# A two-layer graph-attention kernel on one core: the second layer's last source scores taken from the first layer's output, its late rows made beside the last matrix products

## The chip, the cores and the metric

The kernel runs on one core of one Trainium2 chip. The metric is the device time of one execution in microseconds (us); lower is better. Of the kernel before, three executions were timed, and one further execution was recorded by the hardware profiler.

## The reference

The input is a graph of N = 1250 nodes and 20,000 random edges, with x of 1250 x 768. Two graph-attention layers run one after the other, then the residual and a layer norm:

```
h = (x @ W).reshape(N, H, C)                 # layer 1: 4 heads of 512; layer 2: 1 head of 768
al_s = einsum(h, a_src); al_d = einsum(h, a_dst)
e = leaky_relu(al_s[src] + al_d[dst], 0.2)   # edges and self loops
m = segment_max(e, dst)                      # over the sources of each target
alpha = exp(e - m[dst]) / (segment_sum(exp(e - m[dst]), dst) + 1e-16)
out = segment_sum(h[src] * alpha, dst) + bias
```

Layer 1 ends with elu, and its output (1250 x 2048) is layer 2's input. The result is layernorm(x + layer 2).

## The kernel before, in words

**Form of the work.** The edges are turned into a dense table of counts C (1250 x 1250). Attention is then dense: for each pair of a source block b (10 blocks of 125 nodes) and a half g of the targets (625 each) a tile of weights P is made, `min(exp(...), 1) * C`, and TensorE accumulates P^T @ [h, 1] in PSUM over b. Such a tile is a *chunk*, number c: chunks 0 to 79 are layer 1 (4 heads x 2 halves x 10), 80 to 99 are layer 2 (80 to 89 the first half, 90 to 99 the second). Float32 products are made of three products of a high and a low part (lines 1726 to 1728, helper `products`), so each chunk passes these steps, with the semaphore that each gives:

- ScalarE `act_relu`: relu(UP * (d + s)) from the target row `drow` and the source's own score (`z_done`)
- GpSimd `pool_add`: plus the shift row `grow` (`e_done`)
- ScalarE `act_exp` (`p_done`), VectorE `dve_counts` (`pc_done`), ScalarE `act_hi` and VectorE `dve_lo` for the two parts (`pt_hi`, `pt_lo`)
- TensorE: 15 pieces of three products.

ScalarE's order is hi(c), exp(c+1), relu(c+2), and in layer 2 also the high part of block c+1 of h2 (`split_h2`). There are three buffers for a chunk in work.

**Order of the heads.** Each engine has its own program, written out by hand, and waits on semaphores; there is no scheduler. In the second half (g = 1) of heads 0 to 2 VectorE also takes the next head's masked maxima (`maxima`, two for each of five chunks) and TensorE makes a block of the next head's h after each chunk. All transfers are issued by SyncE, in one order. The shift of the next head goes through memory: `store_shift` writes `gcol` as a column, and `load_grow` reads it back as a row on all partitions.

**Between the layers (W2 stage).** For each block b of 10: the layer-1 rows come from memory (`load_hb` to `hblk`, two slots); TensorE transposes them in two halves (`transpose_h`), ScalarE and VectorE make the parts `hT`; TensorE multiplies by W2 (`mm_half(2b)`, `mm_half(2b+1)`: 8 steps k of 6 products); ScalarE takes h2 out of PSUM (`h2_out`, line 1167); VectorE takes its source and target scores (`scores2`, line 1520, two instructions with an accumulator, into `al2`). The source score of each block is stored as a column and read back as a row piece of `arow2` (`store_s2`, `load_s2`). With that row VectorE takes the layer's masked maxima: blocks 0 to 3 at once (`maxima2`, line 1530), blocks 4-5, 6-7 and 8-9 in three parts of ten instructions (`part_maxima2`, line 1545, `merge`, line 1553).

**At the end of the W2 stage,** after the last product: h2_out(9), scores2(9), TensorE spreads the score of block 9 over all partitions (`spread`, line 1792: one product with the identity per block of 125), ScalarE copies it (line 1214), the third part of the maxima, `merge`, `dve_shift` (lines 641 to 645), a spread of the 10 target scores (copied by lines 1190 to 1192 to `drow2`), a spread of the shifts (copied by lines 1197 and 1198 to `grow2`), and then chunk 80's steps.

**Layer 2.** TensorE takes chunks 80 to 89 all into the eight banks (`ORDER2`), then waits for target tiles 0 and 1 to be evicted (`evict2`, line 1606, semaphore `y_b`) and takes the second half tile by tile. On VectorE evict2(0) and evict2(1) stand before dve_lo(97). The last steps are layer norms (`norm`, lines 1623 to 1632), and the stores of the output.

## Time and profile before

| what | value |
|---|---|
| median of 3 runs | 937.47 us (936.48 to 937.52) |
| the profiled execution's own time | 937.02 us |
| its span, first to last instruction | 935.1 us |
| mean granted TensorE clock | 0.987 |
| busy: TensorE, VectorE, ScalarE, GpSimd | 881.1, 602.1, 424.4, 198.1 us |
| transfers | 111.18 MB, 119 GB/s on average |

The times above are of whole executions; the profile's span leaves out 1.9 us around them. A busy TensorE means that some product was in flight, not that it ran at its peak. Lines are those of the kernel before. The changed kernel has other line numbers, since lines were added.

### The profile page before, as it was taken

Reading aid. Unit: us, or ns where it says so; the run is one execution under the profiler, and the core shown is the slowest. Engines: PE = TensorE matmul, PEld = TensorE weight load, DVE = VectorE, ACT = ScalarE, POOL = GpSimd, SP = SyncE. Lnnn points to the kernel's source line nnn. Section 1 sums busy time; section 2 is a strip of 40 time slices with the busy share of each in tenths; the row PEclk is TensorE's granted clock in tenths of the full one; section 3 lists DMA queues with packets and bytes.
Section 4 is the critical chain, followed back from the end, with each engine's and each line's share of the span. In section 5 each row is a group of like instructions: output and inputs, shape, how many; then the busy total and the mean of one; then the engine's idle time right before and its main releaser. Section 6 shows DMA issues by size and latency. Waiting matters only on the chain.

```text
span 935.1 us, 15156 instructions
## 1 busy us (share of the span) xinstructions
PE 881.1 (94%) x5719; PEld 796.9 (85%) x5719; DVE 602.1 (64%) x1169; ACT 424.4 (45%) x686; POOL 198.1 (21%) x134
## 2 busy tenths in 40 slices
PE   4998879999999999999999999989999999699996
PEld 2455557799888998889988899989999999599996
DVE  9458663668873889638895488672223334497886
ACT  5456452276643866339652396661111111487300
POOL 1000000144212332124321244300000000155452
PEclk9999989999999999999999999999999999799999
DMA  8609999462548237472174243655223322400223
GB/s 298 145 14 132 178 174 159 135 211 81 177 138 239 67 103 212 112 231 78 29 214 139 68 142 117 174 166 115 72 48 70 85 48 30 102 1 2 69 84 95
DMA packets 64450, 111.18 MB, mean 119 GB/s; under 512 B 31772, under 2 KB 33464, under 8 KB 63004
## 3 DMA queue, kind: packets, MB, share of 16 engines
q1 hardware_dynamic: 64379, 110.22, 45.7%
q8 instruction: 46, 0.75, 0.4%
q14 instruction: 25, 0.20, 0.1%
HBM read 85.25 MB, written 24.94 MB: 118 GB/s over the span
## 4 chain that ended last, share of the span: by engine, by line
PE 67%; DVE 11%; issue 9%; POOL 6%; ACT 3%; DMA 2%; DVEq 1%; SPq 1%; POOLq 0%; ACTq 0%
PE ps L1726 19%; PE ps L1728 19%; PE ps L1727 19%; POOL pbuf L608 5%; PE ps L1755 3%; PE ps L1696 2%; PE ps L1847 2%; PE ps L1686 1%; DVE pbuf L621 1%; DVE h2f L1632 1%; DMA mask_scratch<-nbs 1%; DVE h2f L1606 1%; DVE vbuf L1440 1%; DMA w1f<-in_L_gnn_W 1%; DVE bnst L1623 1%
## 5 line engine op out<-in xcount | busy, mean ns | idle before, releaser
L608 POOL TENSOR_TENSOR pbuf<-pbuf,grow 125x625 f32<-125x625 f32 x100 | 169.9, 1700 | 701.2 <-ACT pbuf L593 261.1
L1726 PE MATMUL ps<-hx,PThi 125*125 125x260 f32 (+5 forms) x800 | 227.3, 284 | 3.0 <-DVE vbuf L1441 2.5
L1728 PE MATMUL ps<-hx,PTlo 125*125 125x260 f32 (+5 forms) x800 | 225.4, 282 | 0.0
L1727 PE MATMUL ps<-hlo,PThi 125*125 125x260 f32 (+4 forms) x800 | 224.9, 281 | 0.0
L1726 PEld LDWEIGHTS ps<-hx,PThi 125*125 125x125 f32 x800 | 148.7, 186 | 7.0 <-DVE vbuf L1441 2.9
L1727 PEld LDWEIGHTS ps<-hlo,PThi 125*125 125x125 f32 x800 | 149.1, 186 | 1.4
L1728 PEld LDWEIGHTS ps<-hx,PTlo 125*125 125x125 f32 x800 | 149.0, 186 | 0.0
L1726 PE MATMUL ps<-W2p,hT 128*125 128x384 f32 x320 | 109.7, 343 | 3.2 <-DVE hT L1453 1.7
L1728 PE MATMUL ps<-W2p,hT 128*125 128x384 f32 x320 | 108.1, 338 | 0.0
L1727 PE MATMUL ps<-W2p,hT 128*125 128x384 f32 x320 | 108.1, 338 | 0.0
L621 DVE SCALAR_TENSOR_TENSOR pbuf<-pbuf,counts 125x625 f32<-125x625 f32 x100 | 90.7, 907 | 25.3 <-ACT pbuf L615 25.2
L630 ACT ACTIVATE PThi<-pbuf 125x625 fp32r<-125x625 f32 x80 | 57.8, 722 | 106.1 <-PE ps L1728 57.0
L615 ACT ACTIVATE pbuf<-pbuf,s_sl 125x625 f32<-125x625 f32 x100 | 81.2, 812 | 48.9 <-POOL pbuf L608 48.8
L635 DVE TENSOR_TENSOR PTlo<-pbuf,PThi 125x625 fp32r<-125x625 f32 x80 | 77.1, 964 | 40.4 <-ACT PThi L630 40.2
L1453 DVE TENSOR_TENSOR hT<-ps,hT 128x500 fp32r<-128x500 f32 x40 | 25.2, 672 | 108.7 <-ACT hT L1129 108.7
L1726 PE MATMUL ps<-h2x,PT 125*125 125x384 f32 (+9 forms) x250 | 77.6, 310 | 6.2 <-DVE PT L635 4.2
L1129 ACT ACTIVATE hT<-ps 128x500 fp32r<-128x500 f32 x40 | 21.2, 586 | 133.0 <-PE ps L1847 133.0
L593 ACT ACTIVATE pbuf<-drow,s_up 125x625 f32<-125x625 f32 x100 | 80.2, 804 | 0.0
L1727 PE MATMUL ps<-h2lo,PT 125*125 125x384 f32 (+7 forms) x250 | 77.3, 309 | 0.0
L1728 PE MATMUL ps<-h2x,PT 125*125 125x384 f32 (+9 forms) x250 | 77.3, 309 | 0.0
L1728 PE MATMUL ps<-W1hi,xr 128*125 128x512 f32 x180 | 71.1, 395 | 0.0
L1726 PE MATMUL ps<-W1hi,xr 128*125 128x512 f32 x180 | 71.0, 395 | 0.0
(186 smaller groups left out, 1571.6 us busy)
## 6 DMA issues: line engine op xcount, KB each, us to landing
xr<-xT_scratch SPq DMA_DIRECT2D x30, 750.0 KB, 4.9
nbm<-mask_scratch SPq DMA_DIRECT2D x40, 273.4 KB
hidden_scratch<-vbuf SPq DMA_DIRECT2D x40, 224.0 KB
hblk<-hidden_scratch SPq DMA_DIRECT2D x10, 896.0 KB
xT_scratch<-xa SPq DMA_DIRECT2D x20, 375.0 KB, 11.7
w1f<-in_L_gnn_W SPq DMA_DIRECT2D x12, 512.0 KB, 9.1
w1raw<-in_L_gnn_W SPq DMA_DIRECT2D x4, 1536.0 KB, 7.9
w2raw<-in_L_gnn_W SPq DMA_DIRECT2D x14, 384.0 KB, 5.4
```

The lines of the kernel that those rows point to most:

```text
L593: act.activation(pslot(c), src[:, g * GN:(g + 1) * GN], ACT.Relu, scale=UP, bias=bias).then_inc(z_done, 1)
L608: pool.tensor_tensor(pslot(c), pslot(c), src[:, g * GN:(g + 1) * GN], ALU.add).then_inc(e_done, 1)
L615: act.activation(pslot(c), pslot(c), ACT.Exp, scale=SLOPE, bias=bias).then_inc(p_done, 1)
L621: dve.scalar_tensor_tensor(pslot(c), pslot(c), 1.0, C[:, b, g * GN:(g + 1) * GN], ALU.min, ALU.mult).then_inc(pc_done, 1)
L630: act.activation(hi_slot(c), pslot(c), ACT.Copy).then_inc(pt_hi, 1)
L635: dve.tensor_tensor(lo_slot(c), pslot(c), hi_slot(c).bitcast(F32), ALU.subtract).then_inc(pt_lo, 1)
L1129: hi = act.activation(ht_part(n % 2, 0, a), PS[:, bank, 0:4 * B], ACT.Copy)
L1453: lo = dve.tensor_tensor(ht_part(n % 2, 1, a), PS[:, bank, 0:4 * B], ht_part(n % 2, 0, a).bitcast(F32), ALU.subtract)
L1726: pe.matmul(dst, ahi, bhi, start=start, stop=False, skip_group_check=shared)
L1727: pe.matmul(dst[:, 0:n], ahi, blo, start=False, stop=False, skip_group_check=shared)
L1728: return pe.matmul(dst, alo, bhi, start=False, stop=stop, skip_group_check=shared)
L1755: t = pe.matmul(win_bank(w), oh_lo[:, bass.ds(at_slot(first, i, v), 1), :].rearrange("p o n -> p (o n)"), ring[:, w % 2, v, 0:win_cols(w)] ...
```

## The change

**In the heads.** W2 times the source vector a_src of layer 2 is a vector of 2048 numbers, w2a: h2's source score is the layer-1 row times w2a. VectorE makes it in 16 pieces (`FOLD2`): in the second half of head 0 and 1 after its other work of chunks b = 0, 1, 5, 8, 9, of head 2 after b = 0, 1, 5, 7, 8, 9. Each piece is one instruction on 128 x 768 (rows of W2 times `as2row`, with an accumulator), and SyncE loads 384 KB of W2 for it into the one buffer `wf2`, waiting for the piece before. After the last piece w2a is stored.

**In the W2 stage.** `prow` is loaded with w2a in three parts (`load_prow`). VectorE takes the source scores of blocks 8 and 9 from `hblk` times `prow` (`late_dots`, six instructions, `late_scores` sums them). TensorE spreads the source scores of blocks 7, 8, 9 before step 6 of mm_half(17), and ScalarE copies them to `arow2`; the stores and loads of scores 7 and 8 through memory are gone. All three parts of the maxima come in VectorE's turn of block 8, the second before `split_hT(19)` and the third after it. `shift2(0)` makes the shifts of the first half; TensorE spreads them before step 3 of mm_half(19). The first half's target row comes through memory.

**At the end.** h2_out(8) waits for the third part of the maxima, since part of `nbp2` and `prow` lie where blocks 8 and 9 of h2 go. Chunk 80's add is made by VectorE from PSUM. h2_out(9) comes after act_hi(80) on ScalarE; TensorE's first chunk waits for h2 blocks 8 and 9 and the copy of the shifts at the pieces that need their banks. The second half's target and shift rows go through memory.

```diff
+FOLD2 = tuple((h, b) for h in range(H - 1) for b in ((0, 1, 5, 8, 9) if h < H - 2 else (0, 1, 5, 7, 8, 9)))
...
+            def load_fold2(h, b):
+                if (h, b) in FOLD2:
+                    i = FOLD2.index((h, b))
+                    if i > 0:
+                        sp.wait_ge(fold2_done, i)
+                    sp.dma_start(wf2[:], W2[128 * i:128 * i + 128, :]).then_inc(ld_fold2, 16)
...
+                    load_fold2(h, (5, None, 7, None, 8)[t])
                 store_shift(h + 1)
                 load_grow(h + 1, 0)
                 load_xr(h + 1, NB - 2)
+                load_fold2(h, 9)
...
+            for b in range(NB - 3):
+                load_hb(b + 3)
+                sp.wait_ge(al2_done, 2 * b + 1)
+                store_s2(b, b + 1)
+                if b == NB - 4:
+                    load_prow(1)
+                sp.wait_ge(s2_stored, RS * (b + 1))
+                load_s2(b, b + 1, ld_s2[max(0, b // 2 - 1)])
...
+                if b == 5:
+                    load_prow(0)
...
+            load_prow(2)
+            sp.wait_ge(ht_ps, 2 * NB - 2)
+            load_part(1)
+            sp.wait_ge(dot_done, 2 * len(PP) + 1)
+            load_part(2)
...
+                    if b == NB - 2:
+                        act.wait_ge(bc2_ps, 1)
+                        act.activation(arow2[:, (NB - 3) * B:N], PS[0:B, 6, 0:3 * B], ACT.Copy).then_inc(bc2_sb, 1)
                     split_hT(2 * b + 3)
-                h2_out(b)
-
-
-            act.wait_ge(h2_sb, NB)
+                if b == NB - 2:
+                    act.wait_ge(mx_last, QP * NB)
+                if b < NB - 1:
+                    h2_out(b)
...
+                if g == 1 and (h, b) in FOLD2:
+                    i = FOLD2.index((h, b))
+                    dve.wait_ge(ld_fold2, RS + 16 * (i + 1))
+                    dve.wait_ge(fold2_done, i)
+                    dve.scalar_tensor_tensor(wf2junk[:], wf2[:], 1.0, as2row[:], ALU.mult, ALU.mult, accum_out=w2a[:, i:i + 1]).then_inc(fold2_done, 1)
...
+                if b == 6:
+                    late_dots(0)
+                if b == 7:
+                    late_dots(2)
+                    late_scores()
...
+                    if n == 2 * NB - 3 and k == LATE_S:
+                        pe.wait_ge(dot_done, 2 * len(PP) + 1)
+                        pe.wait_ge(ht_lo, 2 * NB - 1)
+                        spread(lambda m: al2[:, 0, m:m + 1], lambda m: (6, (m - NB + 3) * B), NB - 3, NB).then_inc(bc2_ps, 1)
+                    if n == 2 * NB - 1 and k == LATE_G:
+                        pe.wait_ge(g_done, H + 1)
+                        spread(lambda m: gcol[:, H * NB + m:H * NB + m + 1], four_from(4), 0, GT).then_inc(bc2_ps, 1)
```

**Where the instructions stand, TensorE.** The rows below are TensorE's program from the last product of the W2 stage in the kernel before (a row is line, operation, output<-inputs and size, and what it waits for; al2 holds the scores, gcol the shifts, h2x and h2lo the parts of h2).

```order
L1728 MATMUL ps<-W2p_127,hT1_133 125x384
L1792 MATMUL ps<-ident_50,al2_67 125x125 [waits al2_done] x2
L1792 MATMUL ps<-ident_50,al2_67 125x125 x9
L1792 MATMUL ps<-ident_50,gcol_66 125x125 [waits g_done]
L1792 MATMUL ps<-ident_50,gcol_66 125x125 x9
L1726 MATMUL ps<-h2x_158,PT2_3_160 125x256 [waits pt_lo,h2_lo,g2_sb,h2x_one]
```

In the changed kernel the two spreads that are left stand inside mm_half(17) and mm_half(19); this is the one inside mm_half(19), between steps 2 and 3:

```order
L1833 MATMUL ps<-W2p_131,hT1_137 125x384
L1897 MATMUL ps<-ident_50,gcol_66 125x125 [waits g_done]
L1897 MATMUL ps<-ident_50,gcol_66 125x125 x4
L1831 MATMUL ps<-W2p_131,hT1_137 125x384
L1832 MATMUL ps<-W2p_131,hT1_137 125x384
```

So 21 spread products after the last W2 product became 3 and 5 between W2 products, and the last W2 product is now followed by chunk 80's first.

**ScalarE, from its last h2_out on.** Before (hT, arow, drow, grow, pbuf are as in the text above, PT is a chunk's high part):

```order
L1167 ACTIVATE h2f<-ps 125x768 [waits h2_ps] x2
L1214 ACTIVATE arow_154<-ps 125x125 [waits bc2_ps,h2_sb]
L1216 ACTIVATE s_up<-al_67 125x10 [waits al2_done]
L1217 ACTIVATE s_sl<-al_67 125x10
L1190 ACTIVATE drow_145<-ps 125x500 [waits bc2_ps]
L1191 ACTIVATE drow_145<-ps 125x500
L1192 ACTIVATE drow_145<-ps 125x250
L593 ACTIVATE pbuf_146<-drow_145,s_up 125x625 [waits pt_lo,s2_up_sb,d2_sb]
```

And now, from the copy of the three spread scores to the third chunk's relu:

```order
L1228 ACTIVATE h2f<-ps 125x768 [waits h2_ps,mx_last]
L1265 ACTIVATE s_up<-al_67 125x10 [waits dot_done]
L1266 ACTIVATE s_sl<-al_67 125x10
L608 ACTIVATE pbuf_155<-drow_154,s_up 125x625 [waits ld_drow0,pt_lo,s2_up_sb]
L608 ACTIVATE pbuf_155<-drow_154,s_up 125x625 [waits pt_lo]
L1272 ACTIVATE h2x<-ident 125x10x2 [waits h2_ps,h2_sb]
L1262 ACTIVATE h2x<-h2f 125x768
L630 ACTIVATE pbuf_155<-pbuf_155,s_sl 125x625 [waits e_done]
L1277 ACTIVATE grow_153<-ps 125x500 [waits bc2_ps]
L1278 ACTIVATE grow_153<-ps 125x125
L645 ACTIVATE PT_1_162<-pbuf_155 125x625 [waits pc_done]
L1228 ACTIVATE h2f<-ps 125x768 [waits h2_ps]
```

Chunk 80's relu, exp and high part (L608, L630, L645) now stand ahead of the last h2_out (the second L1228), where before they stood behind it.

**VectorE, from the end of the maxima on, in the changed kernel:**

```order
L1613 TENSOR_TENSOR mx<-mx,mxp 125x10 [waits mx_all,mx_last]
L1641 SCALAR_TENSOR_TENSOR mneg<-mx,al_67 125x5 [waits al2_done,mx_all]
L1643 SCALAR_TENSOR_TENSOR negm<-mneg 125x5 [waits m_neg]
L1645 SCALAR_TENSOR_TENSOR gcol<-negm,al_67 125x5 [waits m_sb]
L1579 SCALAR_TENSOR_TENSOR a2junk,al_67<-h2f,a2row 125x768 [waits al2_done,h2_sb]
L1686 TENSOR_TENSOR pbuf_155<-pbuf_155,ps 125x500 [waits bc2_ps,z_done]
L1687 TENSOR_TENSOR pbuf_155<-pbuf_155,ps 125x125
L1682 TENSOR_TENSOR h2lo<-h2f,h2x 125x768 [waits h2_hi]
L636 SCALAR_TENSOR_TENSOR pbuf_155<-pbuf_155,counts 125x625 [waits p_done]
L650 TENSOR_TENSOR PT_1_162<-pbuf_155,PT_1_162 125x625 [waits pt_hi]
L1579 SCALAR_TENSOR_TENSOR a2junk,al_67<-h2f,a2row 125x768 [waits al2_done,h2_sb]
L1641 SCALAR_TENSOR_TENSOR mneg<-mx,al_67 125x5 [waits al2_done,mx_all]
```

Chunk 80 is finished here ahead of block 9's target score (the last L1579), which is followed by the shifts of the second half.

## Rows read from the trace of the kernel before

**Rows 1.** The page's busy times and its chain that ended last, by engine.

```profile
PE 881.1 (94%) x5719; PEld 796.9 (85%) x5719; DVE 602.1 (64%) x1169; ACT 424.4 (45%) x686; POOL 198.1 (21%) x134
...
PE 67%; DVE 11%; issue 9%; POOL 6%; ACT 3%; DMA 2%; DVEq 1%; SPq 1%; POOLq 0%; ACTq 0%
```

**Rows 2.** Windows: busy us (instructions) by engine, granted clock, DMA share, GB/s.

```profile
785.00:799.00 14.00, 13.94 (x80) 13.62 (x78) 5.52 (x35) 0.02 (x1) 0.00 (x0) 1.00 0.21 18
799.00:815.00 16.00, 8.44 (x42) 7.77 (x42) 8.76 (x41) 8.24 (x18) 2.75 (x2) 0.79 0.47 124
```

**Rows 3.** Timeline, PE, 798 to 874: start us, us, operation [idle before <-releaser].

```profile
798.61 0.34 PE L1728 MATMUL ps<-W2p,hT 128*125 128x384 f32 x1
...
801.72 4.08 PE L1792 MATMUL ps<-ident,al 125*125 125x125 f32 x20 [0.40 <-DVE a2junk L1520]
...
815.87 0.55 PE L1726 MATMUL ps<-h2x,PT 125*125 125x256 f32 x1 [4.19 <-DVE PT L635]
```

**Rows 4.** Timeline, ACT, 782 to 816 (same columns).

```profile
798.98 0.81 ACT L1167 ACTIVATE h2f<-ps 125x768 f32<-125x768 f32 x1 [15.12 <-PE ps L1728]
...
814.68 0.80 ACT L615 ACTIVATE pbuf<-pbuf,s_sl 125x625 f32<-125x625 f32 x1
```

**Rows 5.** Timeline, POOL: the add of chunk 82.

```profile
816.26 1.52 POOL L608 TENSOR_TENSOR pbuf<-pbuf,grow 125x625 f32<-125x625 f32 x1 [3.00 <-ACT pbuf L593]
```

**Rows 6.** Timeline, PE, 180 us: ten spread products (two records each).

```profile
180.33 2.42 PE L1792 MATMUL ps<-ident,gcol 125*125 125x125 f32 x20 [1.04 <-DVE gcol L645]
```

**Rows 7.** Timeline, DVE: split_hT(19), then the second part of the maxima.

```profile
783.19 1.27 DVE L1453 TENSOR_TENSOR hT<-ps,hT 128x500 fp32r<-128x500 f32 x2 [5.14 <-ACT hT L1129]
...
786.13 0.41 DVE L1545 CUSTOM_DVE_ANT_0 junk<-nbp,arow 125x250 bf16<-125x250 bf16 x1
...
790.77 0.17 DVE L1553 TENSOR_TENSOR mx<-mx,mxp 125x10 f32<-125x10 f32 x1
```

**Rows 8.** Timeline, DVE: a score of block 7, and the first of block 9.

```profile
766.64 0.95 DVE L1520 SCALAR_TENSOR_TENSOR a2junk<-h2f,a2row 125x768 bf16<-125x768 f32 x1
...
799.82 0.96 DVE L1520 SCALAR_TENSOR_TENSOR a2junk<-h2f,a2row 125x768 bf16<-125x768 f32 x1 [8.88 <-ACT h2f L1167]
```

**Rows 9.** Timeline, SP: block 6's scores as a column, then back as a row.

```profile
748.15 0.74 SPq L852 DMA_DIRECT2D score_scratch<-al  x2
757.31 0.74 SPq L858 DMA_DIRECT2D arow<-score_scratch  x2
```

**Rows 10.** Timeline, DVE: evict2(0) begins.

```profile
869.87 0.15 DVE L1594 TENSOR_SCALAR deps<-ps 125x1 f32<-125x1 f32 x1
```

**Rows 11.** Timeline, PE: the second half's first product.

```profile
873.14 0.46 PE L1726 MATMUL ps<-h2x,PT 125*125 125x384 f32 x1 [1.99 <-DVE h2f L1606]
```

**Rows 12.** Waits, 190 to 640: us in total, times, longest us.

```profile
ACT PThi L630 <- PE ps L1728: 57.0, 21, 3.1
...
PE ps L1726 <- DVE PTlo L635: 0.3, 1, 0.3
```

**Rows 13.** Windows, the busiest part of a second half-pass (columns as in rows 2).

```profile
244.00:260.00 16.00, 16.00 (x100) 14.20 (x99) 15.73 (x24) 8.30 (x13) 3.70 (x3) 1.00 0.76 232
873.00:877.00 4.00, 3.86 (x13) 3.86 (x14) 3.21 (x4) 1.35 (x2) 3.93 (x2) 0.57 0.53 171
```

**Rows 14.** Timeline, head 2's second half: DVE, SP, POOL, DVE, ACT.

```profile
487.54 2.04 DVE L1447 SCALAR_TENSOR_TENSOR vbuf<-ebuf,vbuf 125x512 f32<-125x512 f32 x1
...
500.95 0.93 SPq L723 DMA_DIRECT2D shift_scratch<-gcol  x2
509.46 0.76 SPq L717 DMA_DIRECT2D grow<-shift_scratch  x2
...
513.72 1.53 POOL L608 TENSOR_TENSOR pbuf<-pbuf,grow 125x625 f32<-125x625 f32 x1 [16.38 <-DMA grow<-shift_scratch]
...
517.32 0.69 DVE L1339 TENSOR_TENSOR hlo<-ps,hx 125x512 fp32r<-125x512 f32 x1 [0.37 <-ACT hx L995]
...
524.17 0.73 ACT L630 ACTIVATE PThi<-pbuf 125x625 fp32r<-125x625 f32 x1 [3.02 <-PE ps L1728]
```

216 lines of the change are left out of this document (136 added, 80 removed).

## The prediction

> **What bounds the kernel now.** First the page: TensorE has work in flight for 94% of the span and holds 67% of the chain that ended last [rows 1]. Whatever is gained must come from where it has none. Second the windows: from 799 to 815 us TensorE is busy for 8.44 of 16 us at a granted clock of 0.79, the one long hole outside the start, and right before it for 13.94 of 14 [rows 2]. Third the timeline of that hole: the last W2 product starts at 798.61, then come spreads and waits, the last of them 4.19 us for the first chunk, whose first product starts at 815.87 [rows 3]. The spreads run slow there: 20 records take 4.08 us, and 2.42 at 180 us [rows 3, 6]; the granted clock of 0.79 is a mix of the full 2.4 GHz and the lower level of 1.2 [rows 2].
>
> Then I ask what ends last behind the hole. TensorE takes the first half of layer 2 from 815.87 until 871.15 (873.14 less the 1.99 of idle), and waits for evict2(1) [rows 3, 11]. On VectorE the evictions stand at a fixed place, before dve_lo(97), and evict2(0) begins at 869.87, when TensorE has long left that tile [rows 10]. So **the start of the second half is set by the chunk loop of ScalarE, GpSimd and VectorE, not by TensorE's first half**; from there to the end every engine follows. An earlier first product alone is worth nothing beyond that: the chunk loop has to begin earlier. Its periodic part begins with chunk 82's add on GpSimd, at 816.26 [rows 5]; chunk 97's evictions follow 53.6 us later. That distance stays: same instructions, same three buffers.
>
> **The change, part by part.**
>
> *1. What stands between the last W2 product and chunk 82's add.* Before: h2_out(9) starts on ScalarE at 798.98, the add at 816.26, 17.28 us later [rows 4, 5]. After: ScalarE does h2_out(9), exp(81), relu(82), and GpSimd adds; chunk 80 is done before. Before, the score starts 0.84 after h2_out's start (799.82 less 798.98) [rows 4, 8], which I take for the step to exp(81) as well; from exp(81) to the add it is 816.26 − 814.68 = 1.58 [rows 4, 5]. So 2.42 us instead of 17.28: **14.86 gained**.
>
> *2. What the W2 stage gains in length.* Three and five spread products inside mm_half(17) and mm_half(19), at the clock of their neighbours: ten blocks take 2.42 at full clock [rows 6], eight take 1.94. **1.94 lost.** Bounds: at the slow pace of the first spread it would be 8/10 of 4.08, 3.3 [rows 3]; the low end is 1.9, since the work itself is needed.
>
> *3. Waits for those spreads.* Scores: the six dots and their sum come when VectorE is idle for 5 us at a time (before split_hT(19) it sat 5.14 [rows 7]). I cost them at nothing, and their cover is nearly 10 us: block 7's second score starts at 766.64 and takes 0.95 [rows 8], late_dots(2) adds two shorter ones: 769.5. Counted back from 798.8 at 13.94/80 = 0.174 us a product [rows 2], two halves of 48, two steps of 6 and some 0.9 of transposes, the spread before step 6 of mm_half(17) stands at 779. This leans on prow(1) and prow(2) landing in time behind block 9's load. A column with that load ahead of it took 748.15 to 757.31, 9.2 us [rows 9]; with 9 us instead of my 3 for each, the cover is gone and the wait is up to about 3 us (late_dots(0) at 757, twice 9, the dots and the sum, against 779).
> Shifts: the three-score copy is there at about 780.5 (779, 0.73 of spread, 0.8 for copy and handoffs). Second part of the maxima: 786.13 to 790.77, 4.64 [rows 7], so here from 780.5 to 785.3 with its merge; split_hT(19), 1.27 [rows 7], starts there instead of at 783.19 (its user, mm_half(19), starts at 791, so over 4 us of cover); third part 4.64, merge and shift2(0) 0.8: 792.1. The spread stands before step 3 of mm_half(19): 798.8 less 30 products, plus the first spread's 0.73, 794.3. **Cover about 2 us, cost nothing**; anything later than that is paid one to one.
>
> *4. Chunk 80.* The second spread is done at 795.5. VectorE's add, exp, counts, high part (beside the copies of the shifts) and low part follow, five steps of some 0.85 each (an exp takes 0.80 [rows 4]): about 799.8, against the end of W2 at 798.95 + 1.94 = 800.9. **TensorE starts at once**, with 1.1 us of cover; were it a little late, the end would not move, since the loop hangs on h2_out(9). Behind h2_out(9) VectorE has scores2(9) (0.96 [rows 8]) and shift2(1) before counts(81): some 0.7 late against the old spacing, while chunk 82's add does not wait for it.
>
> *5. The heads.* 16 instructions of 0.95 us (a score is the same form [rows 8]), 15.2 us of VectorE, and 6.3 MB more. In 190 to 640 us TensorE waited once, 0.3 us, for a low part, while ScalarE waited 57 us for TensorE to free a buffer [rows 12]: VectorE is ahead. I cost them at nothing. The thin spot is head 2: the shift goes out at 500.95, is back at 509.46 and is added at 513.72; the block of h behind it is split on VectorE at 517.32, and TensorE comes for it when chunk 58 is done, about 524.2 (ScalarE's buffer wait ends then) [rows 14]. The loads of pieces 14 and 15 stand ahead in SyncE's queue, the former behind a wait for VectorE; I make the delay 4 to 5 us, with 6.6 of cover.
> In the same stretch a 512-column instruction took 2.04, where another of that width takes 0.69 [rows 14]: 1.35 more. At 2.3 a piece, 16 make 37 us instead of 15.2, and the four among maxima would leave VectorE up to 5 us behind; that is the first rival's upper end, and for that I give it 0.05 more. The Trainium skill, "SBUF — State Buffer", section "Who interferes with whom", has it that a VectorE instruction with two SBUF inputs and a GpSimd one that reads SBUF contend for a shared pair of ports, and the one that comes second waits for the other to end. The trace agrees with it in that row.
>
> *6. Second half.* TensorE now finishes its first half at 800.9 + 55.3 − 1.5 (no slow clock at its start) = 854.7, and VectorE lets it go on at 873.14 − 12.9 = 860.2: it idles 5.5 us instead of 2. After 1.99 idle the clock stood at 0.57 for 873 to 877 [rows 13], so that loss is paid already; I take the same loss after the longer gap; no row shows it, and twice the loss, 1.6 us more, is my bound.
>
> **Sum:** 14.86 − 1.94 = 12.9 us. Against the profiled execution's 937.02: 924.1; the median of the runs lies 0.45 above that execution: **924.6**.
>
> **Rivals.**
> - *The folds cost TensorE something.* Loads and port waits push head 2's shift past its 6.6 us, or a piece of W2 lands late and VectorE stands before a needed low part. For it: VectorE is busy 15.73 of 16 us in 244 to 260 [rows 13], where b = 5 falls. Against: VectorE is ahead [rows 12]. 1 to 5 us back: 925.6 to 929.6. Chance 0.15.
> - *A spread comes late in the W2 stage* (point 3): 1 to 5 us: 925.6 to 929.6. Chance 0.10.
> - *TensorE sets the end after all:* if the loop runs faster than before and VectorE reaches its evictions by 854.7, the gain is 871.15 − 854.7 = 16.4: 921.0. Against: the loop's add-exp-relu circle has no part that the change shortens. Chance 0.05.
> - *Slower:* VectorE becomes the engine that sets the pace of the second half-passes, and all 16 pieces are paid. It decides once VectorE has no idle time left per chunk and is no longer ahead; the row of 244 to 260 comes near that, but only 4 of the 16 pieces lie in chunks with maxima. 924.6 + 15.2 = 939.8. Chance 0.03.
> - *It does not do what it says:* a wait in SyncE's single queue (block 9's load, dots, prow, maxima) closes in a row, and chunk 80 begins where it did: 936 to 937.5. Chance 0.02.
>
> **Numbers.** The forecast has 0.65. A measurement of this kernel tells about 0.2% (1.9 us) from no change: faster 0.95, same 0.02, slower 0.03. Range: from 921.5 (most of the faster rival, and 3 us for a step I priced too high) to 929.5 (both rivals of late waits).
>
> **What would show it.** h2_out(9) at about 801 and chunk 82's add 2.4 us behind it; TensorE's first layer-2 product within 0.5 us of its last W2 product, at full clock; no wait at the two spreads; evict2(0) near 857; TensorE idle for about 5.5 us before the second half; low parts still ahead in the heads, chunk starts there unmoved. Wrong if TensorE waits over 1 us for gcol or for the scores, or if mm_half(0) starts later than before.

## The result, and the profile after

The changed kernel takes 926.65 us, median of 4 runs (925.62 to 928.05), against 936.98 of the kernel before (4 runs, 936.31 to 937.52) in the same comparison: a ratio of 0.988, 95% interval [0.986, 0.99]. Two later comparisons gave 0.9882 [0.9859, 0.9906] and 0.9866 [0.9838, 0.9894]. Its profiled execution took 926.86 us, its span 924.8 (before: 937.02 and 935.1). The forecast of 924.6 is 2.05 us too low.

First the page's busy times and its chain that ended last, the lines that answer to [rows 1].

```profile
PE 876.1 (95%) x5693; PEld 792.6 (86%) x5693; DVE 621.3 (67%) x1215; ACT 422.2 (46%) x681; POOL 205.3 (22%) x133
...
PE 69%; DVE 11%; issue 8%; POOL 6%; ACT 3%; DMA 1%; DVEq 1%; SPq 0%; POOLq 0%; ACTq 0%
```

Then windows in the columns of [rows 2]: the end of the W2 stage, and what was the hole. TensorE is busy for all of the first, at full clock, and for 11.40 of 12 us in the first chunks of layer 2, where [rows 2] had 8.44 of 16 at 0.79. The third window is the beginning of the second half.

```profile
785.00:799.00 14.00, 14.00 (x85) 14.00 (x85) 10.60 (x56) 4.76 (x10) 0.00 (x0) 1.00 0.00 0
803.00:815.00 12.00, 11.40 (x95) 11.18 (x94) 11.20 (x13) 10.09 (x14) 5.92 (x3) 1.00 0.07 2
861.00:867.00 6.00, 4.22 (x13) 4.22 (x14) 5.92 (x8) 1.39 (x2) 4.54 (x3) 0.50 0.39 128
```

The timeline of TensorE (start us, us, operation [idle before <-releaser]), as in [rows 3]: the score spreads (six records), the shift spreads, the last W2 product, the first product of layer 2, the wait for chunk 81, and the second half's first product.

```profile
780.85 0.82 PE L1897 MATMUL ps<-ident,al 125*125 125x125 f32 x6
...
796.08 1.25 PE L1897 MATMUL ps<-ident,gcol 125*125 125x125 f32 x10
...
802.26 0.34 PE L1833 MATMUL ps<-W2p,hT 128*125 128x384 f32 x1
802.43 0.28 PE L1831 MATMUL ps<-h2x,PT 125*125 125x256 f32 x1
...
808.57 0.38 PE L1831 MATMUL ps<-h2x,PT 125*125 125x256 f32 x1 [0.60 <-DVE PT L650]
...
862.78 0.68 PE L1831 MATMUL ps<-h2x,PT 125*125 125x384 f32 x1 [5.64 <-DVE h2f L1712]
```

Neither spread waits, and the first product of layer 2 starts 0.17 us after the last W2 product starts. Next are ScalarE, GpSimd and VectorE, for [rows 4, 5, 10]. The first ScalarE row is h2_out(9), the GpSimd row is chunk 82's add, and the last VectorE row is evict2(0). The VectorE rows before it are the wait for prow(1), the sum of the scores, the last step of shift2(0) and the low part of chunk 80:

```profile
802.63 0.81 ACT L1228 ACTIVATE h2f<-ps 125x768 f32<-125x768 f32 x1 [1.85 <-PE ps L1833]
803.48 0.82 ACT L630 ACTIVATE pbuf<-pbuf,s_sl 125x625 f32<-125x625 f32 x1
804.20 0.81 ACT L608 ACTIVATE pbuf<-drow,s_up 125x625 f32<-125x625 f32 x1
...
805.08 1.90 POOL L623 TENSOR_TENSOR pbuf<-pbuf,grow 125x625 f32<-125x625 f32 x1 [3.56 <-ACT pbuf L608]
...
767.05 0.96 DVE L1627 SCALAR_TENSOR_TENSOR a2junk<-hblk,prow 125x768 bf16<-125x768 f32 x1 [5.21 <-DMA prow<-folded_scratch]
...
775.25 0.16 DVE L1633 TENSOR_REDUCE al<-bnst 125x2 f32<-125x6 f32 x1
...
793.64 0.17 DVE L1645 SCALAR_TENSOR_TENSOR gcol<-negm,al 125x5 f32<-125x5 f32 x1
...
800.81 1.37 DVE L650 TENSOR_TENSOR PT<-pbuf,PT 125x625 fp32r<-125x625 f32 x1 [0.80 <-ACT PT L645]
...
859.52 0.15 DVE L1700 TENSOR_SCALAR deps<-ps 125x1 f32<-125x1 f32 x1
```

From h2_out(9) to chunk 82's add it is now 805.08 − 802.63 = 2.45 us, where [rows 4, 5] have 17.28. Yet evict2(0) comes only 10.35 us earlier (859.52 for 869.87), and that is not all the loop's doing: the first shifts' spread, in a stretch that the change does not touch, starts here at 182.45, 2.12 us later than in [rows 6]. It has to be known whose these 2.12 us are before anything else is counted.

**One reference point.** In every trace that follows I count from the first eviction of head 0, a VectorE row of form 125x260 that stands near 227 us in all kernels and that the change leaves alone. Three landmarks behind it: the last such eviction of the heads, evict2(0), evict2(2) (the third eviction of the last stage), and the span's end. All numbers are differences of starts in one trace.

| profiled execution | first head eviction at | last head eviction | evict2(0) | evict2(2) | end |
|---|---|---|---|---|---|
| kernel before | 227.54 | +385.12 | +642.33 | +654.33 | +707.56 |
| changed | 229.69 | +384.89 | +629.83 | +641.91 | +695.11 |
| changed, e4_changed_again | 225.59 | +384.85 | +629.82 | +641.92 | +695.11 |
| changed, e12_changed_base | 230.19 | +384.84 | +629.77 | +641.86 | +695.11 |

Behind the reference point three executions of the changed kernel agree to 0.06 us; ahead of it they differ by 4.6. Counted so, the change gains 12.50 us at evict2(0) and 12.45 at the end.

### The profile page after: what moved, and what is told of

Same layout as the page of the kernel before. It is cut to its first block, busy times and chain, and to the rows that moved or that the text cites. A ratio compares the mean times of both kernels' runs of the same rounds, so it can differ in the third digit from the quotient of the medians.

```text
span 924.8 us, 15200 instructions
## 1 busy us (share of the span) xinstructions
PE 876.1 (95%) x5693; PEld 792.6 (86%) x5693; DVE 621.3 (67%) x1215; ACT 422.2 (46%) x681; POOL 205.3 (22%) x133
## 4 chain that ended last, share of the span: by engine, by line
PE 69%; DVE 11%; issue 8%; POOL 6%; ACT 3%; DMA 1%; DVEq 1%; SPq 0%; POOLq 0%; ACTq 0%
PE ps L1831 19%; PE ps L1833 19%; PE ps L1832 19%; POOL pbuf L623 6%; PE ps L1860 4%; PE ps L1801 3%; PE ps L1952 2%; PE ps L1791 1%; DVE h2f L1738 1%; DVE pbuf L636 1%; DVE h2f L1712 1%; DMA w1f<-in_L_gnn_W 1%; DVE bnst L1729 1%; DVE vbuf L1495 1%; DVE vbuf L1494 1%
## 5 line engine op out<-in xcount | busy, mean ns | idle before, releaser
L623 POOL TENSOR_TENSOR pbuf<-pbuf,grow 125x625 f32<-125x625 f32 x99 | 177.1, 1790 | 683.0 <-ACT pbuf L608 244.3
L630 ACT ACTIVATE pbuf<-pbuf,s_sl 125x625 f32<-125x625 f32 x100 | 81.3, 813 | 59.0 <-POOL pbuf L623 56.9
L636 DVE SCALAR_TENSOR_TENSOR pbuf<-pbuf,counts 125x625 f32<-125x625 f32 x100 | 88.2, 882 | 28.5 <-ACT pbuf L630 28.3
L645 ACT ACTIVATE PThi<-pbuf 125x625 fp32r<-125x625 f32 x80 | 57.8, 722 | 107.1 <-DVE pbuf L636 64.5
L650 DVE TENSOR_TENSOR PTlo<-pbuf,PThi 125x625 fp32r<-125x625 f32 x80 | 83.5, 1043 | 28.2 <-ACT PThi L645 28.2
L608 ACT ACTIVATE pbuf<-drow,s_up 125x625 f32<-125x625 f32 x100 | 80.3, 805 | 0.0
## 6 DMA issues: line engine op xcount, KB each, us to landing
xT_scratch<-xa SPq DMA_DIRECT2D x20, 375.0 KB, 10.4
```

What stands on the lines that cost most here:

```text
L608: act.activation(pslot(c), src[:, g * GN:(g + 1) * GN], ACT.Relu, scale=UP, bias=bias).then_inc(z_done, 1)
L623: pool.tensor_tensor(pslot(c), pslot(c), src[:, g * GN:(g + 1) * GN], ALU.add).then_inc(e_done, 1)
L630: act.activation(pslot(c), pslot(c), ACT.Exp, scale=SLOPE, bias=bias).then_inc(p_done, 1)
L636: dve.scalar_tensor_tensor(pslot(c), pslot(c), 1.0, C[:, b, g * GN:(g + 1) * GN], ALU.min, ALU.mult).then_inc(pc_done, 1)
L645: act.activation(hi_slot(c), pslot(c), ACT.Copy).then_inc(pt_hi, 1)
L650: dve.tensor_tensor(lo_slot(c), pslot(c), hi_slot(c).bitcast(F32), ALU.subtract).then_inc(pt_lo, 1)
```

## The experiments

Times of whole runs differ by several us from execution to execution, so the effects of 0.3 to 4 us below are read in the landmarks; the timed ratio stands beside each. The three comparisons ran with medians of 938.05, 939.95 and 937.53 us for the kernel before.

**e4_changed_again and e12_changed_base** are the changed kernel without an edit.

> The changed kernel itself once more, timed beside the kernel before, as the base of the other runs of this call. If the 2.1 us that its profiled execution had lost by the first shifts' spread (182.45 against 180.33 us) is the execution's own, the spread stands elsewhere this time by up to 2 us and the whole later trace with it; if it belongs to the program, it stands at 182.4 +- 0.3 us. Ratio to the kernel before 0.988 +- 0.002 either way.

> The changed kernel once more, as the base of the runs of this call on their chip. Counted from the first head eviction (near 227 us) its landmarks are those of the two traces of it so far to 0.2 us: first eviction of the last stage +629.8, third +641.9. What lies ahead of the first head eviction may differ by some us, as in the runs so far (the first shifts' spread at 178.2 to 184.8 us).

Measured 925.6 us, ratio 0.9882 [0.9859, 0.9906], and 925.5 us, 0.9866 [0.9838, 0.9894]. The first shifts' spread starts at 178.38 and 182.98. So the 2.12 us are the execution's own. Over all fourteen traces of this study that spread lies between 178.16 and 184.84, whichever kernel it is. The windows show one difference that goes with it: the stretches in which TensorE's clock was granted below full. First the changed kernel, then e4:

```profile
60.00:80.00 20.00, 16.84 (x105) 11.94 (x104) 11.82 (x43) 11.36 (x25) 0.00 (x0) 0.91 0.37 69
...
120.00:140.00 20.00, 12.89 (x74) 8.79 (x72) 13.00 (x44) 11.44 (x24) 0.00 (x0) 0.91 1.10 195
140.00:160.00 20.00, 19.17 (x90) 14.92 (x91) 6.53 (x20) 4.88 (x9) 0.00 (x0) 0.83 0.73 149
```

```profile
60.00:80.00 20.00, 16.64 (x119) 11.88 (x117) 13.56 (x49) 12.21 (x27) 0.00 (x0) 1.00 0.41 68
...
120.00:140.00 20.00, 12.77 (x73) 8.55 (x72) 15.06 (x50) 10.41 (x21) 0.00 (x0) 0.89 1.10 195
140.00:160.00 20.00, 20.00 (x99) 15.84 (x99) 5.35 (x10) 5.50 (x10) 0.00 (x0) 0.94 0.99 164
```

The six other windows of 20 us up to 180 are at 1.00 in both. An estimate from these rows: 20 us times what the clock lacks of full, summed up to 180 us, is 7.0 us in the changed kernel and 3.4 in e4, where the spread comes 4.07 us earlier. Over the fourteen traces this sum goes from 3.4 (spread at 178.16 to 180.47) to 10.4 (184.84). So the late starts go with a longer time at the lower clock, but it is not all: five traces besides e4 have the same 3.4, the kernel before among them, and they differ by 2.3 us. This is read from the rows and not tested; what makes the clock fall there, and what the rest is, stays open.

**e1_folds_alone**: the kernel before with the folds only.

```diff
+                load_fold2(h, 0)
...
+                if g == 1 and (h, b) in FOLD2:
+                    i = FOLD2.index((h, b))
+                    dve.wait_ge(ld_fold2, RS + 16 * (i + 1))
+                    dve.wait_ge(fold2_done, i)
+                    dve.scalar_tensor_tensor(wf2junk[:], wf2[:], 1.0, as2row[:], ALU.mult, ALU.mult, accum_out=w2a[:, i:i + 1]).then_inc(fold2_done, 1)
```

> The kernel before with the first part of the change alone: the 16 loads of W2 rows, the 16 products of them with the source vector on VectorE in the heads, and the store of the folded column. Nothing reads the result, so all else is the kernel before. Theory (the folds lie in cover): the head evictions of the heads (the 125x260 ones, at 227.54 to 608.73 us in the kernel before) keep their places to 0.3 us but for one constant that is there before the first fold, and the time is the kernel before's, 0 +- 1 us. Rival (the folds cost TensorE in the heads): the evictions drift later from head to head, +1 to +15 us by 608.73. Rival for the 2.1 us by which the changed kernel is late already at the first shifts' spread (182.45 against 180.33 us): if the larger program or the placing of its buffers does it, the spread stands at 182.4 here too; if it is the run's own, it stands anywhere from 180 to 183.

Measured 936.7 us, ratio 0.999 [0.9972, 1.0007]. First head eviction 226.21, last +385.09, evict2(0) +642.64, end +707.89. The heads are as before (+385.12), and so is the start of the last W2 product (+571.04 for +571.07). The 0.3 us are lost behind it: layer 2's first product comes at +588.65 for +588.33. The folds as placed cost TensorE nothing in the heads, and the spread at 178.99 says again that the program is not what makes the start late.

**e7_folds_twice**: how much more VectorE could take.

```diff
-                    dve.wait_ge(fold2_done, i)
-                    dve.scalar_tensor_tensor(wf2junk[:], ...)
+                    for j in range(2):
+                        dve.wait_ge(fold2_done, 2 * i + j)
+                        dve.scalar_tensor_tensor(wf2junk[:], ...)
```

> The changed kernel with each of the 16 folds done twice on VectorE (the second writes the same numbers). VectorE was busy 340.5 of the 450 us from 190 to 640 and gets 16 more of 0.96 to 1.9 us. Theory (the folds lie in VectorE's idle time, and its lead on TensorE absorbs what does not): head evictions at the same distances from the first shifts' spread to 0.3 us, time within 0.5 us of the changed kernel; TensorE's waits for the low parts from 190 to 640 us stay under 1 us. Rival (the single folds had used up the lead): +2 to +16 us, seen as drift from one head eviction to the next.

Measured 928.27 us, ratio 0.9894 [0.9864, 0.9923]. Last head eviction +389.21: 4.3 us later than +384.89, so my theory is refuted at twice the number, and the rival holds in its lower half. Waits from 190 to 640 us (us in total, times, longest), of the changed kernel and then of e7:

```profile
ACT PThi L645 <- PE ps L1833: 42.5, 14, 3.1
...
DVE wf2junk L1550 <- DMA wf<-in_L_gnn_W: 9.0, 6, 3.2
...
PE ps L1831 <- DVE PTlo L650: 0.3, 1, 0.3
```

```profile
ACT PThi L645 <- PE ps L1834: 18.2, 6, 3.1
...
PE ps L1832 <- DVE hlo L1393: 3.3, 4, 2.1
...
PE ps L1832 <- DVE PTlo L650: 0.3, 1, 0.3
```

The row to look at is not the low parts of the chunks, on which the prediction had rested: it stays at 0.3 us. A new one is there: TensorE, about to make the next block of h, waits 3.3 us in all for VectorE to have split the block before it (hlo). The longest of the four waits is in head 2's second half, at the thin spot that point 5 of the prediction names:

```profile
525.94 0.50 PE L1832 MATMUL ps<-W1hi,xr 128*125 128x512 f32 x1 [2.07 <-DVE hlo L1393]
```

The four waits make 3.3 of the 4.3 us; the last us was not followed. ScalarE's wait for TensorE to free a buffer, the measure of how far the helpers are ahead, goes from 57.0 [rows 12] over 42.5 with 16 folds to 18.2 with 32. The single folds had used a part of the lead, and no wait for hlo is in the changed kernel's trace.

**e6_shift_spread_last**: the five shift spreads behind the last W2 product.

```diff
-                    if n == 2 * NB - 1 and k == LATE_G:
-                        pe.wait_ge(g_done, H + 1)
-                        spread(lambda m: gcol[:, ...], four_from(4), 0, GT).then_inc(bc2_ps, 1)
...
                 t.then_inc(h2_ps, 1)
+                if n == 2 * NB - 1:
+                    pe.wait_ge(g_done, H + 1)
+                    spread(lambda m: gcol[:, ...], four_from(4), 0, GT).then_inc(bc2_ps, 1)
```

> The changed kernel with the five spreads of the shifts behind the last W2 product instead of beside the last block: what their place among the products is worth by itself. Theory: the last product ends 1.25 us earlier, the spreads end at about 802.6 us (on the changed kernel's clock of events), VectorE's add of chunk 80 begins at 802.8 instead of 797.44, its exp at 803.7, its high part at 805.4, and the last output copy, which ScalarE has behind them, at 806.1 instead of 802.63; chunk 82's add at about 808.5 instead of 805.08. So +3.4 us (3.0 to 3.8) at the first eviction of the last stage. Rival (the end of the W2 products sets the start, not chunk 80): -1.25 to 0 us. Rival by the old arrangement, in which 14.8 us were lost behind the last output copy: over +6 us, which would say that the place of the spreads is most of the gain.

Measured 929.39 us, ratio 0.989 [0.9863, 0.9917]. evict2(0) +633.59, 3.76 later than in the changed kernel; end +698.95, 3.84 later. TensorE's spreads and its first layer-2 product, ScalarE's exp(80), in e6:

```profile
803.63 1.25 PE L1897 MATMUL ps<-ident,gcol 125*125 125x125 f32 x10
809.79 0.55 PE L1831 MATMUL ps<-h2x,PT 125*125 125x256 f32 x1 [4.91 <-DVE PT L650]
...
805.89 0.82 ACT L630 ACTIVATE pbuf<-pbuf,s_sl 125x625 f32<-125x625 f32 x1 [7.18 <-DVE pbuf L1687]
...
808.22 0.79 ACT L1228 ACTIVATE h2f<-ps 125x768 f32<-125x768 f32 x1
```

ScalarE waits 7.18 us for chunk 80's sum, h2_out(9) stands behind chunk 80's high part, and TensorE is idle for 4.91. The chain is the one expected, 0.4 us longer.

**e9_both_spreads_last**: the score spreads too.

```diff
-                    if n == 2 * NB - 3 and k == LATE_S:
-                        pe.wait_ge(dot_done, 2 * len(PP) + 1)
-                        pe.wait_ge(ht_lo, 2 * NB - 1)
-                        spread(lambda m: al2[:, 0, m:m + 1], ...).then_inc(bc2_ps, 1)
...
                 if n == 2 * NB - 1:
+                    pe.wait_ge(dot_done, 2 * len(PP) + 1)
+                    spread(lambda m: al2[:, 0, m:m + 1], ...).then_inc(bc2_ps, 1)
                     pe.wait_ge(g_done, H + 1)
```

with the row copy on ScalarE and part_maxima2(1) on VectorE behind their split_hT(19).

> The changed kernel with both sets of spreads, the three score rows and the five shift rows, behind the last W2 product. VectorE's part maxima 1 and 2, which read the score rows, then lie behind it too. The row copy on ScalarE and the parts on VectorE are moved behind the last splits, so that the last half block's operands don't wait for them. What the place of the score spreads is worth by itself, beside e6_shift_spread_last (+3.8 us). Theory (the chain score rows, part maxima, shifts, shift rows, chunk 80 lies bare behind the last product): last product at about 800.5 us on the changed kernel's clock of events, score spreads 0.8, row copy 0.5, two parts of 4.65 and their merges, shifts 0.6, shift spreads 1.25, so that VectorE's add of chunk 80 begins at about 813.5 instead of 797.44 and chunk 82's add at about 819 instead of 805.08: +14 us (13 to 15) at the first eviction of the last stage, of which 10 are the score rows'. Rival (most of the gain is that less work is done at all, the products of the last rows being gone): under +8 us.

Measured 941.34 us, ratio 1.0042 [1.0022, 1.0062]: slower than the kernel before. evict2(0) +646.21, 16.4 later than in the changed kernel, where 14 were expected.

```profile
798.68 0.82 PE L1897 MATMUL ps<-ident,al 125*125 125x125 f32 x6
810.67 2.46 PE L1897 MATMUL ps<-ident,gcol 125*125 125x125 f32 x10 [11.17 <-DVE gcol L1645]
818.04 0.55 PE L1831 MATMUL ps<-h2x,PT 125*125 125x256 f32 x1 [4.91 <-DVE PT L650]
...
810.45 0.17 DVE L1645 SCALAR_TENSOR_TENSOR gcol<-negm,al 125x5 f32<-125x5 f32 x1
```

The place of the score rows is worth 16.4 − 3.8 = 12.6 us, that of the shift rows 3.8. Of the 2.4 us over what was expected 1.2 are in one row: the five shift spreads (ten records) take 2.46 us here behind 11.17 us of idleness, and 1.25 in e6. e9 is not the old order, though: it has two parts of the maxima behind the last product, where the kernel before had one. The part that is added takes 4.9 us here (800.25 to 805.15), and without it evict2(0) would stand at about +641.3, an estimate, for the +642.33 of the kernel before. Since e9 does only the work of the changed kernel, by this estimate what fell away (13 of 21 spread products) is worth about 1 us, and the rest of the 12.5 us is the order. The folds matter because they make the last scores known before the last products.

**e5_shift_spread_first and e11_score_spread_first**: what a wait inside the W2 stage costs. The diff is e5's; e11 has `0, 3`.

```diff
-LATE_S, LATE_G = 6, 3
+LATE_S, LATE_G = 6, 0
```

> The changed kernel with the five spreads of the shifts ahead of the last half block of W2 products instead of behind three of its steps (3 x 1.06 us). In the changed kernel's trace the shifts are ready at 793.8 us and the last half block begins at about 792.9, so the spreads have a cover of 2.3 us where they stand, and would have to be waited for by 0.9 us here. Theory (TensorE sets the end of the W2 stage, and a wait in it is paid one to one): TensorE idles 0.8 to 1.0 us before these spreads, and the last output copy, chunk 82's add and the first eviction of the last stage all come 0.8 to 1.0 us later, counted from the first shifts' spread near 180 us. Rival (ScalarE's and VectorE's work on chunk 80, which begins 1.4 us earlier here, sets the start of layer 2): 0 or down to -1 us.

Measured 926.0 us, ratio 0.9859 [0.9832, 0.9885]; evict2(0) +630.99, 1.16 later. The wait is the one expected:

```profile
792.05 1.32 PE L1897 MATMUL ps<-ident,gcol 125*125 125x125 f32 x10 [0.88 <-DVE gcol L1645]
```

> The changed kernel with the three score spreads at the begin of their half block of W2 products instead of behind six of its steps (6 x 1.06 us). In the changed kernel's trace the scores are ready at 775.4 us and the bank that the spreads write is read until 777.07, the spreads begin at 780.85, so the cover is 3.8 us, and at the begin of the half block (774.43) the spreads would have to be waited for by 2.6 us. Theory (a wait of TensorE in the W2 stage is paid one to one): TensorE idles 2.4 to 2.8 us before the score spreads, and the first eviction of the last stage comes 2.4 to 2.8 us later. Rival (the cover is the 10 us that the forecast gave, or the wait is taken up again by the rows being there earlier): 0 to 0.5 us.

Measured 931.14 us, ratio 0.9921 [0.9895, 0.9948]; evict2(0) +637.43, 7.6 later and not 2.6. TensorE's spreads and VectorE's first dot on prow(1), then the windows behind the spreads:

```profile
781.40 1.59 PE L1897 MATMUL ps<-ident,al 125*125 125x125 f32 x6 [4.78 <-DVE hT L1507]
...
771.73 0.96 DVE L1627 SCALAR_TENSOR_TENSOR a2junk<-hblk,prow 125x768 bf16<-125x768 f32 x1 [6.59 <-DMA prow<-folded_scratch]
```

```profile
782.00:793.00 11.00, 11.00 (x53) 11.00 (x53) 6.39 (x46) 0.48 (x1) 0.00 (x0) 0.77 0.32 76
793.00:806.00 13.00, 13.00 (x80) 12.96 (x79) 7.05 (x38) 4.45 (x9) 0.00 (x0) 1.00 0.00 0
```

Two things were missing in my sum. In this execution prow(1) is issued at 762.52 and used at 771.73, 9.2 us instead of 7.8 (759.23 to 767.05); the issue itself is 1.3 us later too, with the reference point's 1.95 taken off. VectorE's queue behind it is later against TensorE's stage: the split that reads the bank which the spreads are to write begins 4.40 us behind TensorE's transposes (780.00 and 775.60) instead of 2.15 (775.81 and 773.66), so the wait is 4.78 us and not 2.6. And behind that wait the clock is granted at 0.77 for 11 us, in a stretch that [rows 2] and the changed kernel pass at full clock; the spreads themselves take 1.59 instead of 0.82. Of the 7.6 us 4.78 are the wait and 0.77 the slower spreads; the slow stretch gives most of the 2.05 that are left (0.23 of 11 us is 2.5, with the end of the spreads in it). In these two runs a wait in this stage is paid at least one to one: 1.16 us for 0.88, and 7.6 for 4.78.

**e2_evict_early**: does TensorE's second half set the end?

```diff
-                if c == CHUNKS + 2 * NB - 3:
+                if c == CHUNKS + 2 * NB - 4:
                     evict2(0)
                     evict2(1)
```

> The changed kernel with the evictions of the first two blocks of the last stage, which free the banks for the second half of layer 2, one chunk earlier in VectorE's order (before the low part of chunk 96 instead of chunk 97). Theory (VectorE's own queue sets the end from there on: its low part of chunk 99, then evictions and norms back to back from 871.6 us to the end): TensorE's second half begins 2 to 3.2 us earlier, at about 859.6 to 860.8 us instead of 862.78, the low part of chunk 99 and the third eviction stay at 871 to 872 us, and the time changes by 0 to -0.5 us. Rival (the begin of the second half on TensorE sets the end): -2 to -3 us.

Measured 925.43 us, ratio 0.9877 [0.9854, 0.99]. TensorE's second half starts at 857.64, +630.05 from the reference point; in the changed kernel it is 862.78, +633.09. That is 3.04 us earlier, and its idle time is down from 5.64 to 2.56:

```profile
857.64 0.68 PE L1831 MATMUL ps<-h2x,PT 125*125 125x384 f32 x1 [2.56 <-DVE h2f L1712]
```

evict2(2) comes at +641.64, 0.27 us earlier, the end 0.20 earlier. So 3 us of TensorE's time before its second half are worth 0.2 us at the end; VectorE's place is what counts. From evict2(2) to the end of the span it is 53.2 us in both kernels (707.56 − 654.33 and 695.11 − 641.91). VectorE's evictions and norms fill it but for ten waits of some 0.67 us for GpSimd's `rstd` and the last 3 us of the output's store, the same in both.

**e3_exp_first, e8_combined, e10_combined_2**: where the loop starts.

```diff
             act_hi(act, CHUNKS)
+            act_exp(act, CHUNKS + 1)
+            act_relu(act, CHUNKS + 2)
             h2_out(NB - 1)
             act.wait_ge(h2_sb, NB)
-            act_exp(act, CHUNKS + 1)
```

is e3 (and the loop leaves that relu out). e8 adds e2's edit and moves `scores2(NB - 1)` and `shift2(1)` from ahead of VectorE's loop to the end of chunk 81's pass. e10 has them earlier:

```diff
             dve_lo(dve, CHUNKS)
-            scores2(NB - 1)
-            shift2(1)
...
                     dve_counts(dve, c + 1)
+                if c == CHUNKS:
+                    scores2(NB - 1)
+                    shift2(1)
                 if c + 1 < CHUNKS + NB:
                     split_h2(c + 1 - CHUNKS)
```

> The changed kernel with chunk 81's exp and chunk 82's relu placed ahead of the last block's output copy on ScalarE, which stood idle for 1.85 us before that copy while GpSimd had chunk 81 ready at 801.5 us. Theory (the chain of ScalarE's relu, GpSimd's add and ScalarE's exp sets the pace of the chunk loop, so its second add sets where it starts): GpSimd's add of chunk 82 begins at about 803.1 instead of 805.08 us, the output copy 0 to 0.7 us later, the loop's chain keeps its step of 3.2 to 3.65 us, and the time changes by -1.5 to -2.0 us. Rival (TensorE's last W2 product and the output copy behind it set the start of layer 2): the first eviction of the last stage stays at 859.5 us or moves later by up to 0.5, and the time changes by 0 to +0.5 us.

Measured 924.72 us, ratio 0.986 [0.9837, 0.9884]; evict2(0) +629.64, evict2(2) +641.75: 0.16 to 0.19 us. GpSimd's add of chunk 82 does come 1.9 us earlier, and the next one gives it back:

```profile
801.12 1.29 POOL L623 TENSOR_TENSOR pbuf<-pbuf,grow 125x625 f32<-125x625 f32 x1 [1.64 <-ACT pbuf L608]
806.88 1.54 POOL L623 TENSOR_TENSOR pbuf<-pbuf,grow 125x625 f32<-125x625 f32 x1 [4.47 <-ACT pbuf L608]
...
804.66 0.73 ACT L645 ACTIVATE PT<-pbuf 125x625 fp32r<-125x625 f32 x1 [2.04 <-DVE pbuf L636]
```

ScalarE stands 2.04 us before chunk 81's high part, since VectorE does counts(81) only behind the score and the shifts, and these wait for h2_out(9). Both theory and rival fell: the ring had a second gate.

> A version meant to beat both. On the changed kernel: chunk 81's exp and chunk 82's relu ahead of the last output copy on ScalarE (which alone gave -0.15 us: the add of chunk 82 came 1.9 us earlier, but chunk 81's counts on VectorE lay behind the last block's score and the last five shifts, which wait for the output copy, and the next add came 5.76 us behind it instead of 3.54), so that score and the shifts are moved behind chunk 82's counts too; and the first two evictions of the last stage one chunk earlier (which alone gave -0.28 us at the third eviction). Theory (the ring of relu, add, exp and counts sets the start of the loop, and both of its gates have to go): the add of chunk 83 begins 1.7 to 2.1 us earlier than in the changed kernel, counted from the first shifts' spread, and the third eviction of the last stage 1.8 to 2.3 us earlier. Rival (a third gate appears: the stores of the second five shifts and targets, now later, or TensorE's first products): under 0.7 us.

Measured 923.87 us, ratio 0.9843 [0.9819, 0.9867]; evict2(2) +640.90, 1.01 earlier, the end 0.98 earlier (0.27 and 0.20 of it are e2's edit). Chunk 83's add is 1.9 us earlier (804.52 − 227.47, against 808.62 − 229.69), but GpSimd's add of chunk 85 comes only 5.65 us behind that of chunk 84, where the usual step is 3.4 to 3.65. VectorE there, and GpSimd's add beside it:

```profile
806.97 0.94 DVE L1580 SCALAR_TENSOR_TENSOR a2junk<-h2f,a2row 125x768 bf16<-125x768 f32 x1
...
808.03 1.40 DVE L1642 SCALAR_TENSOR_TENSOR mneg<-mx,al 125x5 f32<-125x5 f32 x1
809.46 0.17 DVE L1644 SCALAR_TENSOR_TENSOR negm<-mneg 125x5 f32<-125x5 f32 x1
...
807.87 1.53 POOL L623 TENSOR_TENSOR pbuf<-pbuf,grow 125x625 f32<-125x625 f32 x1 [1.64 <-ACT pbuf L608]
```

> As e8_combined (-1.01 us at the third eviction of the last stage), but the last block's score and the last five shifts stand between chunk 81's counts and the low part of h2's block 1 on VectorE, where e8_combined left it idle for 1.47 us, instead of behind chunk 82's work, where they held up chunk 83's counts (GpSimd's fourth add came 5.65 us behind the third). Theory: 0.9 to 1.5 us of those 2.8 us fall into the idle stretch, chunk 83's add begins 0.8 to 1.8 us earlier than in the changed kernel, and the third eviction 1.3 to 2.0 us earlier. Rival (VectorE is the bound of the first ten chunks, 3.6 of 3.65 us of each, and the 2.8 us are paid wherever they stand): -0.8 to -1.2 us, as e8_combined.

Measured 923.27 us, ratio 0.9848 [0.9822, 0.9874], beside 925.5 of the changed kernel in the same comparison; evict2(2) +640.65, 1.26 earlier, end +693.88, 1.23 earlier. It lies at the edge between theory and rival: chunk 83's add is 1.8 us earlier, chunk 84's 0.4, and the loop comes out 1.0 ahead of e2. In its first ten chunks VectorE has low part, counts and h2's low part to do, which fill its step of 3.65 us (records of 0.80, 0.80 and 2.13 us that overlap a little, the last beside GpSimd's add), so work put there is mostly paid. e10 is in the traces the fastest of all, by 1.2 us over the changed kernel; the timed ratios of the two overlap.

## Why the prediction was right, by its steps

All differences here are counted from the reference point, between the traces of before and of the changed kernel.

- **What bounds.** Confirmed by e2: the chunk loop's start and VectorE's place for the evictions set the end; 3 us of TensorE's time before the second half are worth 0.27 at evict2(2). The rival "TensorE sets the end after all" is out.
- **1, 14.86 gained.** Measured 17.28 − 2.45 = 14.83. ScalarE's copy to exp(81) took 0.85 and exp(81) to the add 1.60, against 0.84 and 1.58. e6 and e9 show that it is the order: shift spreads put behind the last product cost 3.8, both sets with their maxima 16.4.
- **2, 1.94 lost.** h2_out(9) stands at +572.94 (802.63 − 229.69) for +571.44 before [rows 4], 1.50 later. The W2 stage had begun 0.24 earlier (its first product that waits, +395.93 for +396.17), so the spreads cost 1.74.
- **3, no waits.** True, and with less room than I gave. Shifts: ready at 793.81, spread at 796.08, 2.3 of cover for my 2. Scores: ready at 775.41, spread at 780.85, 5.4 for my 10, and by e11's bank 3.8. The term that was wrong is the load of prow(1): 3 us in the sum, 7.8 measured here and 7.4 to 9.2 over the twelve traces that have it, near the bound from [rows 9]. That it cost nothing was partly luck. VectorE stood before it for 5.21 us. The second took 4.7 at most (769.04 to 773.78); with 9 us for it too, as in my bound, under 1 us of the cover would have been left (778 for its landing, 780 with the two dots and the sum, against 780.85).
- **4, chunk 80 ready 1.1 us before the end of W2.** 800.81 + 1.37 = 802.18. The last W2 product ends at 802.60, and layer 2's first starts at 802.43: 0.25 to 0.4 of cover. From the end of the spread to there it took 4.85 us, for my 4.3. TensorE still starts at once, as said, at full clock.
- **5, the heads cost nothing.** The last head eviction is even 0.23 us nearer (+384.89 for +385.12; the reason was not looked for). The delay of head 2's shift was my thin spot: store, load, add and split, for [rows 14], stand at

```profile
506.46 1.10 SPq L738 DMA_DIRECT2D shift_scratch<-gcol  x2
514.98 0.76 SPq L732 DMA_DIRECT2D grow<-shift_scratch  x2
...
521.07 1.53 POOL L623 TENSOR_TENSOR pbuf<-pbuf,grow 125x625 f32<-125x625 f32 x1 [22.15 <-DMA grow<-shift_scratch]
...
524.68 0.69 DVE L1393 TENSOR_TENSOR hlo<-ps,hx 125x512 fp32r<-125x512 f32 x1 [0.37 <-ACT hx L1056]
```

  With the reference point's 2.15 off, store and load are 3.4 us later than in [rows 14], add and split 5.2; I had 4 to 5, of 6.6 of cover (by [rows 14] 524.17 − 517.32 − 0.69 = 6.2). Little of it was left: the split ends at 525.37, and the product of TensorE that has to come behind it stands at 526.02, 0.65 us later. That this spot held was luck as much as foresight. The rival "the folds cost TensorE" is out for 16 folds (e1) and true for 32 (e7), where the same product, at 525.94, is the one that waits 2.07 us; the low parts of the chunks, by which I had judged VectorE's lead, show nothing of it.
- **6, the second half.** TensorE idles 5.64 us (5.5 forecast), and the clock is 0.50 for 861 to 867, where [rows 13] have 0.57 behind 2 us. From the first product of the half on, the clock is 0.75 over 6.86 us before (873.14 to 880) and 0.70 over 7.22 us now (862.78 to 870), which makes 1.7 and 2.2 us lost: about the same loss, as forecast, and not twice. The end hangs on VectorE.
- **What was not in the sum.** The chunk loop: 53.6 us from chunk 82's add to evict2(0), "that distance stays", measured 54.44: 0.83 lost. The first three steps of GpSimd's adds are 3.54, 3.65 and 3.65 for 3.18, 3.40 and 3.64 before, 0.62 in all; the score and shifts that point 4 has ahead of counts(81), "some 0.7 late", stand there, and e3 shows that they hold up the ring. The prediction says so in point 4 and leaves it out of the sum. The other 0.2 were not followed.

The sum with what was measured: 14.83 − 1.74 − 0.83 + 0.24 = 12.50, against 12.9; that it is so close owes something to errors of opposite sign (0.83 lost, 0.24 and 0.20 gained). The 2.05 us by which the median was missed are mostly no step of the forecast: 0.45 are steps (12.9 for 12.45 at the end), and 2.15 are the late start of this execution of the changed kernel. Against them stand 0.66, since the median lies 0.21 below its profiled execution where the forecast had it 0.45 above. The rest, 0.1, is outside of the span. The two later comparisons, with six executions each, gave medians of 925.6 and 925.5. Of the rivals, the slower one and the one that it does nothing are excluded by the ratio; "a spread comes late" did not happen, and e11 shows that it would have cost more than one to one.

## What to carry to other kernels

A short instruction put into another engine's stage is worth the chain that had to run behind that engine's last work in the old order. Find the input that is known last, and see whether a product taken beforehand (a fold) makes it known earlier, as with the last scores here. Then take the stall away on paper and ask which queue is the next to hold up the end: here moving one gate (e3) gave 0.2 of 1.9 us, and with the second moved too (e10) and e2's edit it was 1.2. And fix a reference point in the trace behind the noisy start before effects of a few us are counted, since three executions of one kernel differed by 4.6 us ahead of it and by 0.06 behind.

## What the runs showed of the hardware

- **A wait of TensorE in a busy stage cost more than its length.** Behind 4.78 us of idleness the next 11 us had a granted clock of 0.77, a mix of 2.4 and 1.2 GHz, and six spread records took 1.59 instead of 0.82 us (e11). Behind 11.17 us ten records took 2.46 instead of 1.25 (e9), about twice as long, at a granted clock of 0.50 from 810.67 to 813.13. Behind 0.88 us the clock stayed at 1.00 from 791 to 795 (e5), and the last stage still came 1.16 us later.
- **A tiny VectorE instruction can take as long as GpSimd's beside it.** The first step of shift2(1), 125x5 with two inputs in SBUF, took 0.17 us in the changed kernel and 1.40 in e8, ending at 809.43, where GpSimd's add of 625 columns ended at 807.87 + 1.53 = 809.40. The Trainium skill, "SBUF — State Buffer", section "Who interferes with whom", has such a pair exclude each other, the second waiting for the first to end; these rows agree to 0.03 us. The next step of the same size, with no add beside it, took 0.17 again, so here it was the neighbour and not the number of columns that set the price.
- **A row loaded to all partitions from a small scratch took 7.4 to 9.2 us** from issue to the first use that waited for it (prow(1), 125x768, twelve traces; 7.8 in the changed kernel), behind other loads. The next one, prow(2) with 512 columns, took at most 4.7.
- **The start is not repeatable.** The same program reached its first head eviction at 225.59, 229.69 and 230.19 us, the earliest with the least time at the lower clock before it.
